# Score passes of wide attention stacked, per-batch work dealt over heads, and late shared blocks in the last mixture

## What is computed

```python
for l in range(4):
    x = x + tanh(g_xattn[l]) * attention_l(layernorm(x), ctx)
    x = x + tanh(g_ffn[l])   * mixture_l(layernorm(x))
```

```python
q = (xn @ w_q).reshape(B, SQ, 16, 64);  k, v = split(ctx @ w_kv)
out = einsum('bhqk,bkhd->bqhd', softmax(einsum('bqhd,bkhd->bhqk', q / 8, k)), v)
return (out.reshape(B, SQ, 1024) @ w_out + b_out) * tanh(gate)
```

```python
gates = top-2 of softmax(x @ router_w)
return expert(x, shared) + sum_e gates[..., e] * expert(x, e) + x
```

## Time and profile before

| | |
|---|---|
| median of 3 runs | 3234.28 us (3232.04 to 3247.9) |
| the profiled execution | 3231.42 us, of which the span of instructions is 3229.6 us |
| granted TensorE clock, mean over the span | 0.885 |
| instructions | 56174 |
| setup and attention 0 / mixture 0 | to about 290 / 570 us |
| attention 1 / mixture 1 | to about 940 / 1366 us |
| attention 2 / mixture 2 | to about 1698 / 2202 us |
| attention 3 / mixture 3 and the end | to about 2736 / 3229.6 us |

### The profile page before, as it was taken

One profiled execution on the slowest core, in us unless ns is written; L12 is line 12 of the kernel. 1 busy time (PEld: TensorE's weight loads), 2 busy tenths in 40 slices (PEclk: granted clock), 3 DMA queues, 4 the chain that ended last, 5 costly groups with the idle time before them and its releaser, 6 DMA issues. The chain is left out here.

```text
span 3229.6 us, 56174 instructions
## 1 busy us (share of the span) xinstructions
PE 2621.8 (81%) x18096; PEld 2400.5 (74%) x18096; DVE 1581.4 (49%) x3623; ACT 1262.4 (39%) x3098; POOL 1254.6 (39%) x1213
## 2 busy tenths in 40 slices
PE   4674479389979999879992689996899897899993
PEld 4574378389968888769992578885788887888882
DVE  3665555366635444346642234434677676343232
ACT  3232134144443333225442334443666565433331
POOL 0012461665322845032205457502544543174313
PEclk9786689698979999969985789998999999899996
DMA  3031244211011533111002234310000000042212
GB/s 113 1 131 47 83 156 132 60 41 34 18 30 47 147 95 112 43 41 34 28 2 62 86 110 135 109 40 30 21 20 13 20 13 27 1 141 89 93 59 88
DMA packets 127510, 205.89 MB, mean 64 GB/s; under 512 B 16401, under 2 KB 88365, under 8 KB 127137
## 3 DMA queue, kind: packets, MB, share of 16 engines
q1 hardware_dynamic: 63232, 117.84, 12.0%
q10 hardware_dynamic: 50208, 47.31, 4.6%
q0 software_dynamic: 13824, 37.53, 3.6%
HBM read 145.58 MB, written 57.02 MB: 63 GB/s over the span
## 5 line engine op out<-in xcount | busy, mean ns | idle before, releaser
L503 ACT ACTIVATE moe_act<-moe_gu 128x256 f32<-128x256 f32 (+1 forms) x431 | 189.3, 439 | 619.2 <-PE moe_gu L95 619.0
L93 PE MATMUL moe_gu<-moe_whi,moe_xThi 128*128 (+2 forms) x1018 | 411.6, 404 | 10.4 <-POOL moe_wlo L294 10.4
L93 PE MATMUL moe_yp<-moe_whi,moe_hThi 128*128 (+1 forms) x1238 | 392.7, 317 | 8.1 <-DVE moe_hTlo L788 7.7
L95 PE MATMUL moe_gu<-moe_whi,moe_xTlo 128*128 (+2 forms) x1018 | 391.7, 385 | 0.0
L94 PE MATMUL moe_gu<-moe_wlo,moe_xThi 128*128 (+2 forms) x1018 | 390.6, 384 | 0.0
L294 POOL TENSOR_TENSOR moe_wlo<-moe_raw,moe_whi 128x768 fp32r<-128x768 f32 (+1 forms) x170 | 341.1, 2007 | 37.2 <-issue 13.8
L94 PE MATMUL moe_yp<-moe_wlo,moe_hThi 128*128 (+1 forms) x1238 | 349.9, 283 | 0.0
L95 PE MATMUL moe_yp<-moe_whi,moe_hTlo 128*128 (+1 forms) x1238 | 349.3, 282 | 0.0
L788 DVE TENSOR_TENSOR moe_hTlo<-moe_tp,moe_hThi 128x256 fp32r<-128x256 f32 (+1 forms) x431 | 210.6, 489 | 238.8 <-ACT moe_hThi L509 237.6
L772 DVE TENSOR_TENSOR moe_h<-moe_act,moe_gu 128x256 f32<-128x256 f32 x321 | 135.0, 420 | 373.5 <-ACT moe_act L503 358.6
L292 POOL CAST moe_whi<-moe_raw 128x768 fp32r<-128x768 f32 (+1 forms) x170 | 152.2, 896 | 300.7 <-DMA moe_raw<-in_moe_w 300.6
(11 more groups left out here) (463 smaller groups left out, 6900.5 us busy)
## 6 DMA issues: line engine op xcount, KB each, us to landing
moe_raw<-in_moe_w SPq DMA_DIRECT2D x118, 384.0 KB, 3.2
moe_raw<-in_moe_w SPq DMA_DIRECT2D x52, 512.0 KB, 4.2
moe_xr<-rows_x ACTq DMA_DIRECT2D x69, 256.0 KB, 2.8
rows_y<-moe_y ACTq DMA_DIRECT2D x69, 256.0 KB, 2.2
rows_x<-att_zeros SPq DMA_DIRECT2D x16, 512.0 KB, 6.7
att_cT_hi<-ctxT_hi SPq DMA_DIRECT2D x24, 256.0 KB, 2.8
att_cT_lo<-ctxT_lo SPq DMA_DIRECT2D x24, 256.0 KB, 3.0
moe_xr<-rows_x ACTq DMA_DIRECT2D x41, 128.0 KB, 2.0
```

The source lines that it names most:

```text
L93: pe.matmul(out, lhs[0], rhs[0], start=first, stop=False, **kw)
L95: return pe.matmul(out, lhs[1], rhs[0], start=False, stop=last, **kw)
L503: act.activation(act_sb[i % 2][:, :], gu[i % 2][:, 0:HC], func).then_inc(act_done, 1)
```

## The change

1. Wide attention. KT is now one tile with a head's high part in partitions 0 to 63 and its low part in 64 to 127. QT[0] holds the queries' high part in both halves, QT[1] the low part above zeros. Two passes a tile make the same three products. Each high-part query is thus written twice by ACT (4 instructions a round, not 2), and keys are split in 64-partition halves (2 and 2, not 1 and 1). Key rounds come before query rounds.
2. Wide and small attention: `take_rows` comes in pieces (K adds, stats, means), in wide attention in heads 7 to 10 and two batches ahead, in the small ones in slots of their own; POOL's roots and norm are pieces too (heads 10 to 15), the fetch stands in head 4. The bias is added ahead of the residual, which waits for it. In the small ones the query tile's first clear and the masks `dg`, `dgc` are DVE's (one broadcast operation each), the first batch's key rounds come earlier, and the biases load before ctx. In wide attention DVE forms batch 0's normalized rows.
3. Mixture 3 has LATE = 6: 10 shared blocks, 39 routed, then 6 shared. The shared weights are loaded again as a tenth set. POOL stores the last routed blocks itself and gathers while the late blocks run, into buffers of its own; DVE adds 1, 4, 7, 10 and 13 tiles by the late blocks' ends and the rest behind them; SP stores x batch by batch, and `final_phase` is gone. Routing takes 8 steps an iteration (was 3).
4. All mixtures with PER: the mask step is one iteration earlier, holds are shorter, and the ranks come after `up`.

```diff
 def moe_phase(...)
+    SE = SJ - LATE
+    RE = SE + NB
+    NX = NE + bool(LATE)
-    NGA = 8
+    NGA = 4 if LATE and glu else 8
-    mask_step = shift_step + 2 + (n_mask - 1) // PER if PER else -1
+    mask_step = shift_step + 1 + (n_mask - 1) // PER if PER else -1
...
+        def is_shared(b):
+            return b < SE or b >= RE
+        def turn_group(b):
+            return NG - 1 if LATE and b + XL == SE else 0
+        def gathered_by(b):
+            return max(0, min(T, 3 * (b - RE + 1) - 5)) if b >= RE else 0
...
+                if out is not None:
+                    for b in range(B):
+                        sp.wait_ge(x_final, TB * b + TB)
+                        sp.dma_start(out[b].rearrange("(t p) d -> p t d", p=P), x[:, TB * b:TB * b + TB, :]).then_inc(out_stored, 16)
...
+                if LATE:
+                    pool.wait_ge(y_copied, NB)
+                    pool.dma_start(rows_y[a:ROWS, :].rearrange("(t p) d -> p t d", p=P), y_sb[q % 2][:, 0:RE - at, :]).then_inc(y_last, 16)
+                    pool.wait_ge(y_last, 16)
...
-                            hold = i + 3
+                            hold = i + 1
...
-                  ... add_input=True, EARLY=1, PER=3)
+                  ... add_input=True, EARLY=1, PER=8, LATE=6, out=out)
 def wide_phase(...)
-    ROUNDS = [(4, "nT", 0), (5, "nT", 1), (6, "qT", 0), (7, "kT", 0), (8, "qT", 1), (9, "kT", 1), (10, "V0", 0), (10, "qT", 2),
-              (11, "kT", 2), (12, "V0", 1), (13, "qT", 3), (14, "kT", 3)]
+    ROUNDS = [(4, "nT", 0), (5, "nT", 1), (6, "kT", 0), (7, "qT", 0), (8, "kT", 1), (9, "qT", 1), (10, "V0", 0), (10, "kT", 2),
+              (11, "qT", 2), (12, "V0", 1), (13, "kT", 3), (14, "qT", 3)]
-        QT, KT = hl("QT", [P, H, S]), hl("KT", [P, 8, S])
+        QT, KT = hl("QT", [P, H, S]), sb("KT", [P, H, S], F32R)
...
-                        mm = mm3(pe, s_ps[q][:, t, :], [a[:, h, t * P:(t + 1) * P] for a in QT], [a[:, h // 2, :] for a in KT], True, True)
+                        for e in range(2):
+                            mm = pe.matmul(s_ps[q][:, t, :], QT[e][:, h, t * P:(t + 1) * P], KT[:, h, :], start=(e == 0), stop=(e == 1))
...
                         for e in range(2):
+                            for a in range(0, P, 64):
+                                ins = act.activation(QT[0][a:a + 64, 4 * part + e:4 * part + 4:2, :], both[64 * e:64 * e + 64], ACT.Copy, scale=-scale)
...
-                        if h == 1 and not last:
-                            take_rows(i + 1)
+                        if 7 <= h < 7 + K + 2 and i < B - 2:
+                            take_rows(i + 2, PIECES[h - 7])
...
+                        if i < B - 2:
+                            if h == 4:
+                                fetch(i + 2)
+                            if h in (10, 11):
+                                roots(i + 2, h - 10)
+                            if h >= 12:
+                                norm(i + 2, h - 12)
 def small_phase(...)
-    TAKE = [-27, -11, *(16 * (b - 1) - 20 for b in range(2, B))]
+    TAKE = {}
+    for b in range(B):
+        for q, piece in enumerate([*range(K), "stats", "means"]):
+            at = (-29, -11)[b] if b < 2 else 16 * (b - 1) - 23 + q
+            TAKE.setdefault(at, []).append((b, piece))
```

422 lines of the change are left out of this document (229 added, 193 removed).

## The result

The median of the changed kernel is 3318.12 us (3310.07 to 3349.0, 4 runs), that of the kernel before 3234.38 (four runs, the three of the table above and one more). The ratio of the runs is 1.0268, with an interval of 1.0193 to 1.0342: slower, where 122 us less were forecast. Its profiled execution took 3349.0 us (span 3347.1), 31 us above the median; the four runs have granted clocks of 0.846, 0.86, 0.855 and 0.86, and the lowest clock belongs to the longest run.

A forecast was written before the change was run, and what follows sets the result against it. TensorE, busy 81% of the span, was taken as the bound. Terms 45 + 14 + 25 + 3 + 2.5 + 5 + 28 = 122.5 us off 3231.42 gave 3108.9; with the median 2.9 above, 3112 us was predicted, range 3072 to 3152.

The forecast's parts named there:

- fall beside the keys' casts and the inverse of the sums, so some of it stays: I take 25: Rotary attention: taking rows in five pieces over five heads shortens PE's six waits, gaining 25 us (ends 12 and 36.6).
- no such stall in its batches: Attention 2 (no rotary, K = 2): no batch stall to remove; only its opening gains, 2.5 us (ends -1.5 and 5).
- The slow-clock rival: Wide attention, heads 7 to 14: new 1 us waits bring PE to 1.2 GHz, 182 us later, 3294 us; chance 0.03.
- PE's head takes (54.5 - 3.8)/16 = 3.2: Wide attention: PE's time per head, 3.2 us, set against ScalarE's 4.1 us in a row in heads 7, 9 and 11.
- The term of 30.1 us for the passes: Wide attention: four passes a head instead of six, 256 fewer over 128 heads at 0.1175 us each, gains 30.1 us.
- The ScalarE rival: Wide attention: ScalarE's added 7.1 us a batch lie on PE's path, waits 8.2 us a batch, 3142 us; chance 0.15.
- 8 + 4 = 12 us: Wide attention: 8 us from waits of 3.9 instead of 5.0 us a batch, and 4 us from batch 0's wait.
- Rotary attention's opening: Start of attention 1: moving POOL's clear and masks to DVE gains 14 us (ends 8 and 16).
- the last mixture: Mixture 3: late shared blocks cover stores, gathers and adds, 41 us gained less two losses, 28 net (ends 12 and 41).
- Its other loss: Mixture 3: loading the shared expert's 2 MB again adds one PE wait for x rows, costing 4 us with its slow clock.
- the second mixture with the opening behind it: Stretch from attention 2's end through mixture 2 and wide attention's opening: forecast 4 us shorter.
- The signs to watch: Profile after: prediction wrong if wide batches exceed 57 us, clock falls in heads 7 to 14, or PE stands over 20 us before the second routed block.

The follow-up runs named there:

- g3: g1 with both small attentions of the change (pieces ahead of normalizing, slots 9 to 13, norm ahead of aux): 3254.23 us, ratio 1.0059 to the kernel before.
- e1: Changed kernel, but in both small attentions DVE normalizes a half batch's outputs before taking the first piece of rows: 3268.68 us.
- e2: Kernel before, plus two scratch DVE operations ahead of normalizing in small attentions, and stacked keys with two passes in wide attention: 3352.0 us, one run.
- g2: g1 with the change's wide attention (stacked keys, ScalarE copies, key rounds first, late residual): 3216.13 us, ratio 0.9958 to the kernel before.
- e5: Changed kernel, normalizing first, later small-attention slots; wide attention six passes, query rounds first, early residual: 3376.26 us, ratio 1.0128; wide stretch 459.3 us.
- e8: Changed kernel, normalizing first; wide attention with six passes, key rounds first and residual early: 3307.61 us; wide stretch 471.2 us.
- g1: Changed kernel with e5's wide attention and small-attention slots, normalizing first, aux ahead of norm: 3151.68 us, ratio 0.9774 to the kernel before.
- f3: Changed kernel with e5's wide attention, rows taken whole in small attentions, mixture 3 with shared blocks first and 3 routing steps: 3228.78 us.
- f4: Changed kernel with both small attentions of the kernel before and e5's wide attention: 3184.1 us, ratio 0.9861 to the kernel before.

## Why the prediction was wrong

**The step that failed most: the pieces "fall beside the keys' casts and the inverse of the sums, so some of it stays: I take 25".** This priced the pieces by what stays of the old waits. It did not ask who waits for what stands behind the piece on DVE, which is the outputs' normalizing, used by PE one slot later. The runs show in its place +103 us for the small attentions (g3; the order of those two alone is 49 us of it in the medians, e1), of which attention 2, for which I had written "no such stall in its batches", is the greater part (341.4 us against 274.8). A stretch without waits over 1 us was taken as safe, and it had the least to lose in waits and the most in clock.

**The slow-clock rival** was the right mechanism in the wrong place. I put it in heads 7 to 14 of wide attention, at 3294 us, with a chance of 0.03, and wrote that waits a third as long as the one of the earlier trace rows spoke against it. The change's median is 3318. Waits of 1.1 us were enough, and in attention 2 the lower level lasted 24 to 31 us, not 8. In wide attention the clock fell too (0.97 to 0.90), and is about half of a batch's miss there: 6.6 us a batch, where the rival had 26. The Trainium skill (TensorE: Matmul & The Clock Gate, A second HAM failure mode: psum-queue depth-cycling) says that small idles of PE between groups of matmuls can make the clock swing; the prediction set it aside on the strength of one wide batch at 1.00. That batch was the exception: the five that follow it in the same trace are at 0.97 and take 61.1 to 61.2 us, each with 3.4 us at the lower level behind POOL's stop. The runs bear the page out for attention 2: e2 brings the swing with two short DVE instructions, e1 takes most of it away by their order.

**"PE's head takes (54.5 - 3.8)/16 = 3.2"** failed in wide attention. The mean hid two kinds of head: those with rounds, 3.28 us, where PE sets the pace and two passes a head fewer show (0.14 to 0.25 us), and those without, 2.15 us, where ScalarE's 1.9 us are nearly all of it. The term of 30.1 us for the passes counted all 128 heads, and is worth 0.14 to 0.25 in a few of each 16; with the 7.1 us of ScalarE's added work, which are needed by the very heads that follow a query round, and the 12 to 18 us of the next paragraph, the whole is +64 us (g2). Most of it falls on head 10, whose two rounds the working never took by themselves: 4.6 of the 7.1 us by which a batch grew. The ScalarE rival named this (3142 us) and priced only its 30 us on top of a gain that did not exist. Its second half, that no gain was there to be taken back, was missing. It also put a batch's waits at 8.2 us, a number for which it names no row; 10.8 were measured.

**A part that was left without a price.** Taking the keys' rounds ahead of the queries' stands in the description of the change and in no term of the sum. It costs 12 us (e5 against e8) to 18. What ScalarE forms for the queries of the next two heads comes later by it.

**Nearly right** are two smaller terms. The work of wide attention that is dealt out was put at 8 + 4 = 12 us and is worth 11 (470.5 before, 459.3 in e5, 457.2 in g1, both with the residual early), though not by the path that I gave: I had subtracted ScalarE's new waits here, which belong to stacking. Rotary attention's opening was put at 14; f3, with a batch's rows whole, gained 12.5 in that stretch.

**Right:** the last mixture (28 forecast, 26 measured; 33 with six passes, g1), and the main path of its mechanism: the end behind PE is 12 us (14.5 forecast), and the first routed block comes 13.0 us late (16 forecast), 9.3 of them for x rows and only 3.7 for the weights that the prediction named. Its other loss, one more wait for x rows by the weights that are loaded again (4 us), didn't come: the other five are 12.9 us, as five were 12.8 before. Right as well are the second mixture with the opening behind it (4 forecast, 2 measured), the price of a pass where PE sets the pace, and that ScalarE's load of a wide batch would not fill it. The signs to watch were right: both the falling clock and wide batches above 57 us were named as what would make the prediction wrong.

**Left open.** What starts a slow stretch and what ends it isn't settled. Late normalizing brings it in every run that has it, but f4, f3, e1 and the change's own last fall show that PE can go to the lower level in attention 2 with no wait in front, and stay there while it is busy. And ScalarE's part in the stacked kernel's heads was measured by moving eight of twelve instructions away; moving the key rounds' four wasn't tried.
